# An adaLN transformer block on one core: the first modulation rows for all batches from one set of products, tile 0 turned by TensorE, constant products during the first load

## What is computed

```python
mod = (silu(c) @ wmod).reshape(4, 6, 1, 512)        # c: (4, 512), wmod: (512, 3072)
sa, ca, ga, sb, cb, gb = mod[:, 0], ..., mod[:, 5]
ga, gb = sign(ga) * max(|ga|, 0.25), sign(gb) * max(|gb|, 0.25)
h = layernorm(x) * (1 + ca) + sa
x = x + ga * linear_attention(h, w_qkv, w_proj, b_proj)   # 16 heads of 32, relu(q), relu(k)
h = layernorm(x) * (1 + cb) + sb
x = x + gb * moe(h)      # 8 experts, 2 per token, inner width 352, and a shared expert of width 704
```

## Time and profile before

| | |
|---|---|
| median of three executions | 1218.91 us |
| lowest and highest of them | 1217.52 and 1221.94 us |
| the profiled execution's own time | 1217.89 us |
| its span, first to last instruction | 1216.1 us |
| its mean granted TensorE clock | 0.996 |
| busy: TensorE | 1189.8 us (98%), 9054 products |
| busy: VectorE | 805.9 us (66%) |
| busy: GpSimd | 506.3 us (42%) |
| busy: ScalarE | 417.7 us (34%) |
| chain that ended last, by engine | PE 90%, DVE 2%, issue 2%, DMA 2% |

### The profile page before, as it was taken

How to read it: one execution, slowest core, us unless ns; L and a number is a source line. 1 busy time by engine, 2 the same in 40 slices (tenths; PEclk the granted TensorE clock), 3 DMA queues, 4 the chain that set the end, 5 groups by cost and what they waited for, 6 DMA issues and landing times.

```text
span 1216.1 us, 25326 instructions
## 1 busy us (share of the span) xinstructions
PE 1189.8 (98%) x9054; PEld 776.8 (64%) x9054; DVE 805.9 (66%) x1578; ACT 417.7 (34%) x873; POOL 506.3 (42%) x409
## 2 busy tenths in 40 slices
PE   7999999999999999999999999999999999999996
PEld 2646666666666666767777777656666666666663
DVE  5647778878776777655857754266666666666665
ACT  4424444445443432333323323222222222222221
POOL 2212566656564554222112112345445554455543
PEclk9999999999999999999999999999999999999998
DMA  7816597998788978745434535579787897779783
GB/s 238 228 40 168 125 250 192 214 234 212 182 222 185 229 209 197 173 99 120 122 87 104 137 85 117 111 150 135 132 141 140 131 132 139 138 135 136 133 127 45
DMA packets 253255, 185.27 MB, mean 152 GB/s; under 512 B 186496, under 2 KB 198784, under 8 KB 253132
## 3 DMA queue, kind: packets, MB, share of 16 engines
q1 hardware_dynamic: 217368, 114.40, 42.1%
q0 software_dynamic: 20512, 45.62, 22.4%
q10 hardware_dynamic: 15256, 23.62, 6.7%
HBM read 87.07 MB, written 52.75 MB: 115 GB/s over the span
## 4 chain that ended last, share of the span: by engine, by line
PE 90%; DVE 2%; issue 2%; DMA 2%; POOL 1%; ACT 1%; SPq 0%; ACTq 0%; POOLq 0%; DVEq 0%
PE ps_o L87 7%; PE ps_o L89 7%; PE ps_o L88 7%; PE ps_vs L87 6%; PE ps_vs L88 6%; PE ps_vs L89 6%; PE ps_kh L87 4%; PE ps_vh L87 4%; PE ps_vh L88 4%; PE ps_vh L89 4%; PE ps_kh L88 4%; PE ps_kh L89 4%; PE ps_qh L87 4%; PE ps_qh L89 4%; PE ps_qh L88 4%
## 5 line engine op out<-in xcount | busy, mean ns | idle before, releaser
L444 POOL DMA_INDIRECT out<-y,slot_row x71 | 139.3, 1963 | 190.3 <-DVE y L882 138.7
L89 PE MATMUL ps_o<-w_all,xt 128*128 x568 | 177.5, 313 | 0.0
L88 PE MATMUL ps_o<-w_all,xt 128*128 x568 | 177.5, 313 | 0.0
L87 PE MATMUL ps_o<-w_all,xt 128*128 x568 | 177.5, 312 | 0.0
L874 DVE SCALAR_TENSOR_TENSOR gate_row<-gate_rows,batch_weight,gate_row 128x512 f32<-128x512 f32 x213 | 158.9, 746 | 2.5
L368 POOL DMA_INDIRECT out<-s_sum,row_no x32 | 53.8, 1680 | 197.6 <-DVE s_sum L623 192.0
L1133 ACT ACTIVATE at<-ps_y 128x384 f16<-128x384 f32 x71 | 34.8, 491 | 250.7 <-PE ps_y L1353 247.1
L330 POOL TENSOR_TENSOR h<-cen,rows_f 128x512 f32<-128x512 f32 x32 | 40.6, 1270 | 130.6 <-ACT cen L901 115.4
L89 PE MATMUL ps_qh<-ht,wqkv 128*128 128x128 f16 x512 | 87.4, 219 | 0.0
L88 PE MATMUL ps_qh<-ht,wqkv 128*128 128x128 f16 x512 | 87.4, 219 | 0.0
L87 PE MATMUL ps_qh<-ht,wqkv 128*128 128x128 f16 x512 | 87.4, 219 | 0.0
(11 more groups left out here) (251 smaller groups left out, 3341.2 us busy)
## 6 DMA issues: line engine op xcount, KB each, us to landing
w_stage<-in_w_d ACTq DMA_DIRECT2D x64, 176.0 KB
xb<-in_x SPq DMA_DIRECT2D x32, 256.0 KB, 3.7
xr<-in_x SPq DMA_DIRECT2D x32, 256.0 KB, 4.0
out<-x SPq DMA_DIRECT2D x32, 256.0 KB, 3.6
h_d<-hl SPq DMA_DIRECT2D x32, 256.0 KB, 2.5
h2t_d<-h2t SPq DMA_DIRECT2D x32, 256.0 KB, 3.5
s_ht<-h2t_d SPq DMA_DIRECT2D x32, 256.0 KB, 3.6
sstage<-in_sh_flat SPq DMA_DIRECT2D x32, 136.0 KB, 3.6
```

What stands on the lines that cost most here:

```text
L87: nc.tensor.matmul(out, lh, rh, start=first, stop=False, skip_group_check=True)
L88: nc.tensor.matmul(out, lh, rl, start=False, stop=False, skip_group_check=True)
L89: return nc.tensor.matmul(out, ll, rh, start=False, stop=last, skip_group_check=True)
L444: pool.indirect_dma_start(m.out, bass.IndirectOffsetOnAxis(ap=m.slot_row[:, t:t + 1], axis=0), m.y[:, t % Y_RING, :], None, compute_op=ALU ...
```

## The change

- VectorE spreads all four batches' columns over 32 columns each, so the same products give the two first parts of all batches, 32 rows for each. They are copied to `modrows`; the store of step 1 reads every 32nd row of it, and `modulate(0)` and `modulate(1)` go. Batch 0's rows are spread to all partitions by two f32 products of a row of ones with row 0 of `modrows` (`ps_row`).
- Tile 0 leaves the common chain: it is centred and scaled by VectorE early, multiplied and shifted from `ps_row` by VectorE, turned by four TensorE transposes, and split in two halves straight into `ht` by ScalarE (`turned_high`) and VectorE (`turned_low`). Its GpSimd add, its `h_high` and `h_low` and its transposing DMA go.
- Before the first load has landed TensorE runs 11 f32 products of a 128x128 tile of ones.
- SyncE's queue issues all twelve pieces (ring of 8 instead of 6); ScalarE issues none. Steps -3 to -1 of VectorE and ScalarE are written out in a new order. TensorE's first projections wait for the weights piece by piece.
- `ident` is made at the start of GpSimd's program instead of in step 0.
- In the expert slots, `e_high(0)` goes ahead of `first_gate_row(0)`; the two halves of `at` are separate buffers, and the wait for the shared expert's last sums moves from slot 0 to slot 1. For the last slot, `e_turn(70)` is done within `e_down(69)`, and `e_low(70)` ahead of `e_out(69)`.

Left out below: the renumbering of `mod` (now parts 2 to 5 only), semaphore names, and the load semaphores of `wmod`.

```diff
-X_RING, QT_RING, HT_RING, XR_RING, X2_RING, H2T_RING, STAGE_RING, W_RING = 4, 10, 3, 2, 3, 3, 6, 4
+X_RING, QT_RING, HT_RING, XR_RING, X2_RING, H2T_RING, STAGE_RING, W_RING = 4, 10, 3, 2, 3, 3, 8, 4
...
-CONSTS = 5
-SPLITS_FIRST = {-2: (4,), -1: (6,), 0: (10, 11)}
-SPLITS_LAST = {-2: (5,), -1: (7, 8, 9)}
+ONE_READY, IDENT_READY, V_READY, HEADS_READY = 1, 4, 6, 11
+WARM = 11
+PE_TURNED = 1
+COPIES = P // B
...
     def turn_h(i):
-        if tile(i):
+        if tile(i) and i >= PE_TURNED:
             sp.wait_ge(m.h_lo, i + 1)
             at_least(sp, m.q_done, i - HT_RING + 1)
             sp.dma_start_transpose(m.ht[:, i % HT_RING, :, :], m.hl[:, i % 2, :, :].rearrange("p s n -> p (s n)")).then_inc(m.ht_loaded[i % HT_RING], 16)
...
@@ -238,7 +243,12 @@
     for n in range(KC):
         sp.dma_start(m.stage[:, n, :], m.pieces[n][0]).then_inc(m.stage_loaded[n], 16)
     load_x(1)
+    for n in range(KC, 2 * KC):
+        sp.dma_start(m.stage[:, n, :], m.pieces[n][0]).then_inc(m.stage_loaded[n], 16)
     load_x(2)
+    for n in range(2 * KC, 3 * KC):
+        sp.wait_ge(m.stage_lo, n - STAGE_RING + 1)
+        sp.dma_start(m.stage[:, n % STAGE_RING, :], m.pieces[n][0]).then_inc(m.stage_loaded[n % STAGE_RING], 16)
...
@@ -324,8 +334,10 @@
             pool.tensor_tensor(m.rstd[:, i % 4, :], m.rstd[:, i % 4, :], m.minus_half[:, :], ALU.pow).then_inc(m.rstd_done, 1)
 
     def shift(i):
-        if tile(i):
+        if tile(i) and i >= PE_TURNED:
             pool.wait_ge(m.scaled, i + 1)
+            if i == PE_TURNED:
+                pool.wait_ge(m.row0_done, 1)
             at_least(pool, m.h_lo, i - 1)
             pool.tensor_tensor(m.h[:, i % 2, :], m.cen[:, i % 2, :], m.rows_f[:, (i // BT) % 2, SA, :], ALU.add).then_inc(m.h_done, 1)
...
+    step(pool.memset(m.one[:, :], 1.0))
     step(pool.memset(m.minus_half[:, :], -0.5))
+    step(pool.memset(m.ident[:, :], 0.0))
+    step(pool.affine_select(out=m.ident[:, :], in_=m.ident[:, :], compare_op=ALU.not_equal, fill=1.0,
+                            base=0, pattern=[[-1, P]], channel_multiplier=1))
     step(pool.memset(m.v_sb[:, :, 0, :, P:P + 1], SCALE))
     step(pool.memset(m.v_sb[:, :, 1, :, P:P + 1], 0.0))
...
-        if s == 0:
-            step(pool.memset(m.ident[:, :], 0.0))
-            step(pool.affine_select(out=m.ident[:, :], in_=m.ident[:, :], compare_op=ALU.not_equal, fill=1.0,
-                                    base=0, pattern=[[-1, P]], channel_multiplier=1))
...
+    def turned_low(half):
+        part = slice(2 * half, 2 * half + 2)
+        v.wait_ge((m.h_half_hi, m.h_hi)[half], 1)
+        v.tensor_tensor(m.ht[:, 0, KC + 2 * half:KC + 2 * half + 2, :], m.ps_first[half],
+                        m.ht[:, 0, part, :], ALU.subtract).then_inc((m.h_half_lo, m.h_lo)[half], 1)
+
     def h_low(i):
-        if tile(i):
+        if tile(i) and i >= PE_TURNED:
             v.wait_ge(m.h_hi, i + 1)
             v.tensor_tensor(m.hl[:, i % 2, 1, :], m.h[:, i % 2, :], m.hl[:, i % 2, 0, :], ALU.subtract).then_inc(m.h_lo, 1)
...
-    for s in range(-3, TILES + TAIL):
+    v.wait_ge(m.silu_done, 1)
+    for k in range(KC):
+        v.tensor_copy(m.sct_rep[:, k, :].rearrange("p (b n) -> p b n", b=B), m.sct[:, k, :].unsqueeze(2).to_broadcast([P, B, COPIES])).then_inc(m.rep_done, 1)
+    stats(0)
+    v.wait_ge(m.rstd_done, 1)
+    v.tensor_scalar(m.cen[:, 0, :], m.xb[:, 0, :], m.mv[:, 0, 0:1], m.rstd[:, 0, :], ALU.subtract, ALU.mult).then_inc(m.cen_done, 1)
+    for n in range(KC):
+        split_low(n)
+    stats(1)
+    v.wait_ge(m.bc_done, 2)
+    v.tensor_scalar(m.modrows[:, C:2 * C], m.ps_o[:, 1, :], 1.0, None, ALU.add).then_inc(m.row_done, 1)
+    split_low(4)
+    v.wait_ge(m.spread_done, 1)
+    v.tensor_tensor(m.h[:, 0, :], m.cen[:, 0, :], m.ps_row[CA], ALU.mult).then_inc(m.scaled, 1)
+    v.wait_ge(m.spread_done, 2)
+    v.wait_ge(m.scaled, 1)
+    v.tensor_tensor(m.h[:, 0, :], m.h[:, 0, :], m.ps_row[SA], ALU.add).then_inc(m.h_done, 1)
+    v.tensor_copy(m.rows_f[:, 0, CA, :], m.ps_row[CA]).then_inc(m.rep_done, 1)
+    v.wait_ge(m.rep_done, KC + 1)
+    turned_low(0)
+    turned_low(1)
+    centre(1)
+    for n in range(5, 9):
+        split_low(n)
+    h_low(1)
+    for n in range(9, 12):
+        split_low(n)
+    k_low(0)
+    stats(2)
+    for s in range(TILES + TAIL):
         t = s - LAG
-        if s == -3:
-            v.wait_ge(m.silu_done, 1)
-            for k in range(KC):
-                v.tensor_copy(m.sct_rep[:, k, :], m.sct[:, k, 0:1].to_broadcast([P, P])).then_inc(m.rep_done, 1)
-        if s == -2:
-            v.wait_ge(m.bc_done, 2)
-            v.tensor_scalar(m.rows_f[:, 0, CA, :], m.ps_o[:, 1, :], 1.0, None, ALU.add).then_inc(m.row0_done, 1)
-            v.wait_ge(m.row0_done, 2)
         q_low(s - 1)
         centre(s + 2)
         centre2(t - 2)
         if 0 < s <= TILES and s % BT == 0:
             key_value_sums(s // BT - 1)
         stats(s + 3)
...
-        if s == -3:
-            for n in range(KC):
-                split_low(n)
-        for n in SPLITS_FIRST.get(s, ()):
-            split_low(n)
...
-        k_low(s)
+        if s > 0:
+            k_low(s)
         h_low(s + 2)
...
@@ -884,27 +914,35 @@
     e_multiply(0)
     add(CHUNKS - 1)
     for t in range(1, SLOT_TILES + 1):
-        e_low(t - 1)
+        if t < SLOT_TILES:
+            e_low(t - 1)
         gate_rows_of(t - 1, 1)
         gate_rows_of(t - 1, 2)
         if t < SLOT_TILES:
             e_multiply(t)
         gate_rows_of(t - 1, 3)
+        if t == SLOT_TILES - 1:
+            e_low(t)
         e_out(t - 1)
...
+    def turned_high(half):
+        part = slice(2 * half, 2 * half + 2)
+        act.wait_ge(m.first_turned, half + 1)
+        act.activation(m.ht[:, 0, part, :], m.ps_first[half], ACT.Copy).then_inc((m.h_half_hi, m.h_hi)[half], 1)
+
     def h_high(i):
-        if tile(i):
+        if tile(i) and i >= PE_TURNED:
             act.wait_ge(m.h_done, i + 1)
-            if i >= 2:
-                act.wait_ge(m.ht_loaded[(i - 2) % HT_RING], ring_use(i - 2, HT_RING))
+            if i >= 2 + PE_TURNED:
+                act.wait_ge(m.ht_loaded[(i - 2) % HT_RING], ht_use(i - 2))
             act.activation(m.hl[:, i % 2, 0, :], m.h[:, i % 2, :], ACT.Copy).then_inc(m.h_hi, 1)
...
@@ -1028,57 +1062,53 @@
 
     act.wait_ge(m.c_loaded, 16)
     act.activation(m.sct[:, :, :], m.ct[:, :, :], ACT.Silu).then_inc(m.silu_done, 1)
-    act.wait_ge(m.wmod_loaded[KC - 1], 16)
-    for n in range(KC, STAGE_RING):
-        load_stage(n)
     for n in range(KC):
         split_high(n)
-    for s in range(-3, TILES + TAIL):
+    act.wait_ge(m.bc_done, 1)
+    act.activation(m.modrows[:, 0:C], m.ps_o[:, 0, :], ACT.Copy).then_inc(m.row_done, 1)
+    split_high(4)
+    split_high(5)
+    turned_high(0)
+    turned_high(1)
+    act.activation(m.rows_f[:, 0, SA, :], m.ps_row[SA], ACT.Copy).then_inc(m.row0_done, 1)
+    scale(1)
+    for n in range(6, 9):
+        split_high(n)
+    h_high(1)
+    split_high(9)
+    split_high(10)
+    k_high(0)
+    split_high(11)
+    for s in range(TILES + TAIL):
         t = s - LAG
-        if s == -2:
-            act.wait_ge(m.bc_done, 1)
-            act.activation(m.rows_f[:, 0, SA, :], m.ps_o[:, 0, :], ACT.Copy).then_inc(m.row0_done, 1)
         logits_out(t - 4)
         q_high(s - 1)
         scale(s + 2)
         scale2(t - 2)
-        if s == -2:
-            load_stage(STAGE_RING)
-            load_stage(STAGE_RING + 1)
-        for n in SPLITS_FIRST.get(s, ()):
-            split_high(n)
         if s == 1:
             act.wait_ge(m.c_loaded, 48)
             act.activation(m.gate[:, :, 0:E], m.gstage[:, :, :], ACT.Copy, scale=SCALE).then_inc(m.stage_hi, 1)
-        k_high(s)
+        if s > 0:
+            k_high(s)
         if s < TILES:
             h_high(s + 2)
             h2_high(t - 2)
-        for n in SPLITS_LAST.get(s, ()):
-            split_high(n)
-            if s == -1 and n < 9:
-                load_stage(n + 3)
-        if s == -2:
-            load_stage(STAGE_RING + 2)
-            load_stage(STAGE_RING + 3)
         v_high(s)
...
-            act.wait_ge(m.mod_done, 1)
-            act.activation(m.mod[:, 0:C], m.ps_y[0:B, :], ACT.Copy).then_inc(m.mod_copied, 1)
...
@@ -1127,10 +1157,10 @@
 
     def e_high(t):
         act.wait_ge(m.at_done, t + 1)
-        if t == 0:
+        if t == 1:
             act.wait_ge(m.s_t1_done, 2 * CHUNKS)
         at_least(act, m.ey_done, t - 1)
-        act.activation(m.at[:, t % 2, 0, :, :], m.ps_a[:, :, :], ACT.Copy).then_inc(m.e_at_hi, 1)
...
@@ -1139,9 +1169,10 @@
         act.activation(m.gate_row[t % GW_RING][:, :], m.gate_rows[:, 0, :], ACT.Copy, scale=m.batch_weight[:, 0, t:t + 1]).then_inc(m.gate_first, 1)
 
     e_silu(0)
-    first_gate_row(0)
     for t in range(1, SLOT_TILES):
         e_high(t - 1)
+        if t == 1:
+            first_gate_row(0)
         first_gate_row(t)
         e_silu(t)
...
@@ -1150,11 +1181,13 @@
```

(43 more changed lines are left out.)

69 lines of the change are left out of this document (35 added, 34 removed).

## The result

The changed kernel takes 1221.89 us (median of 22 runs, 1218.89 to 1223.99), the kernel before 1218.06 us (22 runs). The ratio is 1.0031, with a 95% interval of 1.0024 to 1.0039: 3.8 us slower, where the forecast had 0.7 us less and called that no change. The profiled execution took 1221.72 us, with a span of 1219.9 us.

What follows compares the result with a forecast made beforehand. TensorE, busy for 98% of the span, was taken to bound the kernel. Head 0.6 us later, slots 1.1 and 0.2 earlier: 0.7 us less, 1218.2 us on the scale of the runs' median; range 1213 to 1222.

Steps and rivals of the forecast that it cites:

- the stand: Before tile 0's sum_keys_values: TensorE stands still for 4.7 us, waiting for v_low(0) on VectorE.
- restart: At project_k(1): after the idle time TensorE's clock is down, which costs 1.9 us (0 to 3.1).
- VectorE's list: VectorE's work from centre(1) to centre(2), ahead of v_low(0): 9.6 us, from 20.0 to 29.6.
- The head: Start of the kernel: project_k(1) 1.3 us earlier, less a 1.9 us restart, so 0.6 us later than before.
- The spread is two products, two records each. At the high level...: Tile 0's start: spread products complete at 16.8 and 17.65 us at the high clock; project_k(0) at 19.7, 5.7 us earlier.
- rival A: Clock also falls before the spread, records take 0.86 us each; 1221.3 us with a 3.1 us restart; chance 0.25.
- ScalarE's six loads of step 0 and `v_low(1)` come about as late as before: The step after project_k(1): it gives no room, so TensorE gains next to nothing even with the clock up.
- Slots: First and last expert slots: reordering gains 1.1 us (0 to 1.6) and 0.2 us (0 to 1.3).
- what is late next is `e_turn(1)`: First expert slot: with the 1.6 us wait gone, the second turn comes at 798.1 instead of 799.22, gaining 1.1 us.
- Ones and bound: Very start: the products of ones and the spread of all batches are together worth 1.0 us, not 3.
- Rival B: At sum_keys_values(0): TensorE doesn't wait, as VectorE's and ScalarE's lists are shorter; 1211.8 us; chance 0.12.
- The sum: Whole kernel: 0.6 us later, 1.1 and 0.2 earlier, so 0.7 us less than before.

Runs made afterwards that it cites:

- e2: The changed kernel without the products of ones (WARM = 0): 1222.18 us, ratio 1.0038 to the kernel before.
- e13: The changed kernel with 10 products of ones between the last real product and the spread: 1224.16 us, ratio 1.0042 to the kernel before.
- e14: The changed kernel with its edits of the expert slots undone: 1224.35 us, ratio 1.0038 to the kernel before.
- e6: The changed kernel with ScalarE's ten loads of steps 0 and 1 issued early, in SyncE's prologue: 1219.92 us, ratio 1.0019 to the kernel before.
- e11: The changed kernel with ScalarE's loads issued by SyncE behind tile 2's transposing DMA and the shared rows: 1220.03 us, ratio 1.0018 to the kernel before.
- e3: The changed kernel with 20 products of ones in TensorE's idle time before sum_keys_values(0): 1223.54 us, ratio 1.0045 to the kernel before.
- e4: The changed kernel with tile 0's v conversion (v_high(0), v_low(0)) moved ahead of stats(2): 1222.82 us, ratio 1.0040 to the kernel before.
- e8: e6 with e4's edit, tile 0's v conversion moved ahead: 1216.44 us, ratio 0.9984 to the kernel before.
- e10: e7 without the products of ones (WARM = 0): 1215.23 us, ratio 0.9973 to the kernel before.
- e7: e8 with tile 0's query conversion moved from step 1 to step 0 as well: 1214.77 us, ratio 0.9978 to the kernel before.
- e12: The kernel before with the same ten loads issued early, in SyncE's step -1: 1225.94 us, ratio 1.0060 to the kernel before.
- e9: e7 with 10 products of ones between the last real product and the spread: 1216.82 us, ratio 0.9980 to the kernel before.
- e1: The kernel before with only the change's edits of the expert slots: 1216.81 us, ratio 0.9992 to the kernel before.
- e5: The changed kernel with ScalarE's loads of steps 0 and 1 put behind its shared conversion of the step: 1227.32 us, ratio 1.0078 to the kernel before.
- e15: The kernel before with the loads issued by SyncE behind the shared rows of steps 0 and 1: 1216.76 us, ratio 0.9987 to the kernel before.

## Why the prediction was wrong

**Right: the stand.** TensorE idle from about 30.9 to 35.4 before `ps_vs`, forecast 29.2 to 33.9; 4.5 us long, forecast 4.7; `project_k(1)` at 1.2 GHz with a restart of 1.8 us, forecast 1.9; the last real product at 13.3, forecast 13; the spread at 15.75, forecast 15.8. VectorE's list sets it, as the sum over its instructions had it: from `centre(1)` to `centre(2)` it takes 9.3 us, forecast 9.6. The head was forecast at +0.6 and came out at +3.3 in the profile.

Two readings of the kernel before were off by the mix of two views: the chain's rows start 0.16 us behind the timeline's. By the timeline `project_k(1)` started at 35.66, not 35.82, and `project_k(0)` took 29.70 - 25.41 = 4.29 us, so that the restart cost 1.7 us and not 1.87. The two errors nearly cancel: the head would have been forecast at +0.5.

**The step that failed first: "The spread is two products, two records each. At the high level..."** This was my own rival A, to which I gave 0.25. Spread and transposes took 3.03 and 1.12 us instead of 1.95 and 0.66 (e2), `project_k(0)` came at 21.34 instead of 19.7, the sum at 35.43 instead of 33.9, and it too ran at the low level (1.25 us to `project_k(1)` instead of 0.65). With that `project_k(1)` is 2.2 us behind the forecast, of the 2.7 missing in the head. How much of it is the clock is read from the other kernels: against e2, where spread and transposes ran at the high level, the sum is 1.3 us later, and at `project_v(1)` the four kernels with the fall in the spread are 0.7 to 1.9 us behind the three without.

The argument against A was that the clock fell before "only at the end of the idle stretch". In the trace of the kernel before it hadn't fallen there at all; the granted clock is 1.00 until 25 us and falls when TensorE is back at work at 25.41:

```profile
24.00:25.00 1.00, 0.00 (x0) 1.00 1.21 194
25.00:26.00 1.00, 0.58 (x2) 0.80 0.91 191
```

In the nine profiles that have the products of ones and no bridge, TensorE is idle for 2.2 to 3.0 us ahead of the spread, and the spread takes 3.0 us or more in six of them and 1.95 to 2.2 in three; the transposes behind it ran at the low level in all nine (1.11 or 1.12 us). So a chance of two in three would have been right for the spread, and the transposes should have been priced at the low level outright. The Trainium skill (TensorE: Matmul & The Clock Gate, Part 1) says that the number of slow products varies from run to run of the same kernel; the nine profiles fit that, though they are of different kernels with equal code of TensorE up to there, and so do the 13 of 17 behind the wait for `vk`. The price of A in the time itself isn't shown: e13 took the fall at the spread away and was 1.5 us ahead at `project_v(1)`, but its time can't be told from the changed kernel's, because waits behind the loads took it back.

**The step that failed second: "ScalarE's six loads of step 0 and `v_low(1)` come about as late as before".** The loads did, within 0.9 us (`v_low(1)` came 2.2 us later, with TensorE), but what stands beside them had moved: tile 2's chain was 1.9 us later (its transposing DMA issued at 34.75, not 32.89), the loads 0.9, and so the two changed places. I had asked only whether a transfer is late, not what it now stands behind. In the changed kernel's profile this order cost 0.45 us, in e14's, with the same head, 2.3; moving the loads away (e6, e11) gave back 1.5 us by the ratios of two kernels. The same order with worse waits is in the profiles of e3 and e4 (in e4 the transposing DMA took 11.6 us), and e4's edit wins once the loads are moved (e8).

**Slots.** Forecast 1.1 and 0.2. In the profiled pair it was 0.57 and 0.09; over all profiles the first can't be told from nothing and the second is under 0.1. The term "what is late next is `e_turn(1)`" held, but the first gate row started at 799.85, 0.54 us later than by the shift of the whole (795.33 + 3.98), because its load landed later. Slot 69's multiply was delayed by 0.5, forecast 0.4, with a wait of 0.22 for an earlier scatter that I had not looked at.

**Ones and bound.** The 1.0 us that I gave to the products of ones and the spread of all batches together isn't borne out for the products of ones: without them the spread starts 0.07 us later in e2 and 0.74 later in e10 (against e7), by when the clock rises without them, and no time shows a gain. What is left of the 1.0 us belongs to the common products and VectorE's list. Rival B needed VectorE to save 4.7 us; the way to it was not a shorter list but another order and free queues (e7), and its 1211.8 is 3 us below what that reached.

**The sum.** In the profiles 3.3 (head), 0.7 (clock behind `vk`), -0.57, -0.09 and 0.5 (last landing) make the 3.8 us; forecast was -0.7. The 0.7 and the 0.5 are of the size by which profiles of equal code differ, so they belong to this pair of profiles and are not the change's. Rival A foresaw 2.4 us over the kernel before (1221.3 against 1218.9) and the measured difference is 3.8; it was right on the spread and wrong on its other half, a restart of 3.1 us, which was 1.8. The forecast also took 0.5% as the least that a measurement can tell; the interval of the 22 runs is 0.15% wide. That the measured 1221.89 lies at the edge of the range it had been given is luck: the kernel before was 0.85 us lower beside it (1218.06) than on the scale of the forecast.

## What to carry to other kernels

Where a stand of an engine goes, list every chain that ends within a few microseconds behind it, transfers with the queue that they stand in, before any gain is written down: here the same edit was worth nothing with the loads in the way and 3.5 us with them moved. When a chain shifts by a microsecond, check for each bulk load whether it now goes ahead of a small latency-bound transfer; loads that nobody needs for ten microseconds belong behind it (e11) or well ahead of it (e6), and where they go they meet the next one (e12, e9). A clock that stays up through one idle stretch of 2.5 us is no evidence for the next, nor for the work right behind it: price both cases.

## What the hardware showed beyond expectation

A transposing DMA of one tile takes 3.1 us alone (e6, e7, e11), 4.5 just ahead of four loads of 512 KB on the other queue, and 10.1 to 11.6 just behind them (after, e1 to e5, e13, e14); behind 2 MB on its own queue 7.1 (e15) and behind 4 MB 12.5 (e12). The Trainium skill (DMA: Bandwidth & Descriptors, Queues, rings and completion order) says that an engine goes round its queues a packet at a time. The traces agree in that loads on ScalarE's queue and transfers on SyncE's are under way together; they don't show the order of the packets. What they show is the outcome: the second queue gave the small transfer no quick way past.

Idle stretches of about the same length let TensorE's clock fall at different times: after 2.65 us in e6 the granted clock was 1.00 for the whole spread (1.95 us) and fell in the transposes (0.68 from 18 to 19 us), after 2.46 us in the changed kernel it fell within the spread (0.74 from 16 to 17). After 3.6 us of idle time in e6 the sum still ran at 0.22 us a record and `project_k(1)` fell to 0.63 only 0.5 us into it, where the changed kernel's sum ran at 0.32 from its second record on after 4.5. The fall can come when the engine is at work again: in e9 it came at 20.5 us, 5 us after the bridge, with stretches of 0.8 and 0.9 us between.
